# Taking the moments of two of four norms, a product and four casts off VectorE in a kernel with attention, a state-space block and a mixture of experts

## The chip, the cores and the metric

One core of one Trainium2 chip. The metric is the device time of one execution in microseconds (us). VectorE is called DVE here, ScalarE ACT, GpSimd POOL, TensorE PE and SyncE SP, as in the profile.

## The reference

For B = 8 batches of T = 512 rows with D = 256 numbers, and a context of G = 1024 rows with 192 numbers:

```
x  = x + tanh(g_xattn) * block1(layernorm(x), context)
x  = x + tanh(g_ffn)   * block2(layernorm(x))
block1: scores = (t Wq)(c Wk)^T / sqrt(32), 4 heads; the 32 largest of each row's 1024 are kept,
        softmax over them, mean over the heads, times c Wv -> c_t
        y = layernorm(t) * (1 + gate*scale_in(c_t)) + gate*shift_in(c_t)
        y = s4d(y), a long convolution, done with a DFT; then scale_out, shift_out; xt = t + y
        xt = xt + gelu(layernorm(xt) W1 + b1) W2 + b2;  block1 = layernorm(xt)
block2: logits = h Wg; the best of 8 experts and its sigmoid score
        routed = silu(h*score G_e) * (h*score U_e) D_e ;  shared = silu(h G) * (h U) D ; sum of both
```

## The kernel before, in words

A batch is four groups of 128 rows with four heads each, so attention has 128 steps of a group and a head ("attention step" n, 16 a batch). One attention step is, on PE, two score matmuls into two PSUM banks (L1606, L1607); on DVE, four times MAX8 (the eight largest of 1024) and MATCH_REPLACE8 (strike them out), L1301 to L1312; on ACT, small operations, then two exponentials of 128x1024, of all scores and of what is left after the striking; on POOL, the difference of the two and its sum over the heads (L669, L671, L673).

The rest of a batch is "post": FILM_IN (film from c_t), FOLD and DFT, the spectrum's product on DVE (L1443 to L1446) and POOL, INV, FILM_OUT, norm, UP, gelu, DOWN, norm, residual, norm, GATE (the router's logits), RANK (each row's place in its expert's list), the scatter of the rows to xs_d, and SHARED with SH_DOWN (the shared expert), whose result POOL adds to the output by a DMA with accumulation (L835). Post of batch b runs under the attention of batch b + 1. After batches 2 to 6 POOL computes a table of full tiles of routed rows (`tables`, some 35 small operations, L841 to L865), and 21 such tiles run under the attention that follows and under the last post (`tiles`); the 18 that are left run at the end (`routed`), out of expert weights that by then lie in SBUF. `prep` normalizes the next batch's rows and makes queries and keys.

There are four norms a batch: one in `prep`, three in `post`. DVE takes mean and variance (`moments`: four L1275, four L1278), ACT and POOL make the root with a Newton step, ACT applies it.

Each engine runs its instructions in order. That order is written out by hand: every part is a generator that yields the slot, a number, of its next piece, and `weave` merges the parts of one engine by slot. One batch is 128 slots, an attention step 8 slots, one of DVE's eight operations one slot. `post_at(b)` is 128(b+1); the tables ahead of the kernel (DVE_SPECTRUM, POOL_SH, ACT_SILU, POST_AT and others) hold the slots within a batch. A slot is an order only: what holds an instruction is its semaphores. Pieces of equal slot run in the order of the parts in `weave`.

PSUM banks 4 to 7 are a ring (RING, sorted by PE's slots) that post, prep, finish and tiles share; banks 0 to 3 hold the scores.

Around the change, in the order of the slots of one batch on each engine:
- DVE: moments of prep at 56, of post at 55.6 (from L1448 on), 98.6 and 110.1; the router's first part at 118 (waits for GATE, L1468, and ends in `v_hot`), the second at 120.2 (waits for RANK, L1478, and ends in `v_pos`; the four casts of row numbers, L1485, lie in it); the shared product `big[k] = big[k] * bank`, four times, at 126.3 to 132.3 (L1500).
- PE: GATE 123.5, the first SHARED 124, RANK 125.1 (L1848 to L1851), SHARED up to 133 (L1870, eight uses of a bank, two matmuls each), SH_DOWN 134.9 to 138.3 (L1879).
- POOL: ROUTE 117.8, 120.5 (four scalings, L821), 121.6 (four scatters, L828); attention's sums of steps 14 and 15 at 123.3 and 124; `tables` at 133; the four L835 at 133.3 to 134.5; the next batch's first difference at 133.8.
- The difference of step n must be done before DVE's first MATCH_REPLACE8 of step n + 2 (`taken`).
- POOL's FOLD waits until the four L835 of the batch before have landed. In the tail POOL also issues eight scatters of zeros (L912), which the routed tiles' loads wait for.

## Time and profile before

| what | before |
|---|---|
| median of 3 runs | 1889.0 us (1885.12 to 1889.39) |
| profiled execution, its own time | 1896.48 us |
| its span | 1894.6 us |
| granted clock of PE, mean | 0.832 of full speed |
| DVE busy | 1568.8 us, 83% |
| PE busy | 1431.8 us, 76% |
| POOL busy | 1188.9 us, 63% |
| ACT busy | 1043.2 us, 55% |

The span divides in three: to 264 us the convolution's kernel is computed beside the first attention steps; to 1613 us attention goes on, one batch about every 189 us; from there to the end there is the tail: the last post to 1780 us, and the 18 last tiles of the routed experts. The views below give busy time by stretch, what each engine waited for, and single instructions in order of time. A number in square brackets at the end of a timeline row is idle time of the engine before the row, with what ended it.

### The profile page before, as it was taken

What the parts mean: (1) busy time and instruction counts of PE and PEld (TensorE: products, weight loads), DVE (VectorE), ACT (ScalarE), POOL (GpSimd) and SP (SyncE); (2) the same over time, 40 slices, a digit from 0 to 9 for tenths busy, and PEclk for the clock granted to TensorE, in tenths of its full rate; (3) what the DMA queues carried; (4) which work ended last, traced back from release to release, by engine and by line L of the source; (5) the groups of instructions that cost most, each with busy time, mean ns of one, the idle gap of its engine ahead of it and who ended that gap; (6) DMA issues with size and microseconds to landing.
All of it is one profiled execution on the core that took longest, in us unless ns stands there. A gap on an engine that the chain in (4) does not pass through costs nothing.

```text
span 1894.6 us, 20729 instructions
## 1 busy us (share of the span) xinstructions
PE 1431.8 (76%) x6301; PEld 1032.0 (54%) x6301; DVE 1568.8 (83%) x2300; ACT 1043.2 (55%) x2108; POOL 1188.9 (63%) x1293
## 2 busy tenths in 40 slices
PE   3532455786878677868988888888888888887997
PEld 1321343555455545545757565656565656656696
DVE  7899999998999899989998999899999999201321
ACT  2656554474647464746576647665766565333342
POOL 1588845655765576558765875687668756733422
PEclk8655666886888588869998998899988897998998
DMA  7200011001100110013223231323132201472322
GB/s 231 66 3 3 20 32 34 23 16 47 39 23 17 45 39 23 17 45 100 73 59 84 76 89 31 85 75 89 31 84 67 70 17 56 111 267 84 78 47 26
DMA packets 99219, 114.77 MB, mean 61 GB/s; under 512 B 18786, under 2 KB 77930, under 8 KB 98964
## 3 DMA queue, kind: packets, MB, share of 16 engines
q1 hardware_dynamic: 86964, 98.87, 17.9%
q0 software_dynamic: 12144, 14.58, 4.7%
q8 instruction: 51, 0.84, 0.2%
q14 instruction: 60, 0.49, 0.1%
HBM read 75.08 MB, written 19.58 MB: 50 GB/s over the span
## 4 chain that ended last, share of the span: by engine, by line
DVE 53%; PE 21%; POOL 10%; issue 9%; ACT 5%; DMA 1%; SPq 0%; ACTq 0%; DVEq 0%; POOLq 0%
DVE R L1309 17%; DVE ZB L1312 14%; DVE ZB L1305 6%; DVE R L1301 6%; PE PS L1925 3%; PE PS L1870 3%; PE PS L1780 2%; PE PS L1823 2%; DVE R L1265 2%; POOL ZB L673 2%; POOL ZB L671 2%; ACT ZB L946 2%; DVE R L1275 2%; PE PS L1935 2%; POOL R L841 1%
## 5 line engine op out<-in xcount | busy, mean ns | idle before, releaser
L1309 DVE MAX8 R<-ZB 128x8 f32<-128x1024 f32 x384 | 471.2, 1227 | 12.0
L1312 DVE MATCH_REPLACE8 ZB<-R,ZB 128x1024 f32<-128x1024 f32 x384 | 464.1, 1209 | 0.0
L671 POOL TENSOR_TENSOR ZB<-ZB 128x1024 f32<-128x1024 f32 x96 | 233.5, 2433 | 167.1 <-ACT ZB L946 154.1
L949 ACT ACTIVATE R<-PS 128x512 f32<-128x512 f32 (+6 forms) x378 | 159.9, 454 | 264.9 <-PE PS L1879 59.7
L673 POOL TENSOR_TENSOR ZB<-ZB 128x1024 f32<-128x1024 f32 x96 | 228.1, 2376 | 7.5
L946 ACT ACTIVATE R<-R 128x32 f32<-128x32 f32 (+2 forms) x352 | 95.1, 272 | 204.5 <-DVE R L1309 141.6
L669 POOL TENSOR_TENSOR ZB<-ZB 128x1024 f32<-128x1024 f32 x32 | 77.2, 2411 | 161.6 <-ACT ZB L946 108.3
L1606 PE MATMUL PS<-ZR 97*128 97x512 f32 x128 | 83.9, 656 | 119.6 <-ACT ZB L946 96.1
L1870 PE MATMUL PS<-R 128*128 128x512 f32 x256 | 151.5, 748 | 8.4 <-DVE R L1500 8.4
L1301 DVE MAX8 R<-PS 128x8 f32<-128x1024 f32 x128 | 156.4, 1222 | 1.0 <-PE PS L1607 1.0
L1305 DVE MATCH_REPLACE8 ZB<-R,PS 128x1024 f32<-128x1024 f32 x128 | 155.4, 1214 | 0.0
L952 ACT ACTIVATE R<-R 128x1 f32<-128x1 f32 (+1 forms) x384 | 140.7, 390 | 26.4 <-POOL R L658 21.6
L946 ACT ACTIVATE ZB<-ZB,R 128x1024 f32<-128x1024 f32 x128 | 146.1, 1141 | 8.7 <-DVE ZB L1312 8.7
L946 ACT ACTIVATE ZB<-PS,R 128x1024 f32<-128x1024 f32 x128 | 142.7, 1114 | 4.2
L1823 PE MATMUL PS<-R 128*128 128x256 f32 x512 | 121.7, 391 | 10.1 <-ACT R L949 9.5
L1814 PE MATMUL PS<-R 128*128 128x512 f32 x256 | 124.5, 633 | 6.3 <-ACT R L949 4.1
L1631 PE MATMUL PS<-ZB 128*128 128x192 f32 x512 | 112.2, 384 | 13.7 <-ACT ZB L949 10.8
L1631 PEld LDWEIGHTS PS<-ZB 128*128 128x128 f32 x512 | 106.1, 232 | 21.2 <-issue 10.8
L1823 PEld LDWEIGHTS PS<-R 128*128 128x128 f32 x512 | 99.5, 196 | 27.4 <-ACT R L949 11.1
L1606 PEld LDWEIGHTS PS<-ZR 97*128 97x128 f32 x128 | 28.0, 219 | 152.3 <-ACT ZB L946 78.3
L1870 PEld LDWEIGHTS PS<-R 128*128 128x128 f32 x256 | 58.6, 238 | 77.3 <-issue 65.0
L1898 PE MATMUL PS<-R,ZB 128*128 128x128 f32 x672 | 87.3, 289 | 14.2 <-ACT R L949 8.9
(242 smaller groups left out, 3173.8 us busy)
## 6 DMA issues: line engine op xcount, KB each, us to landing
ZR<-ZR SPq DMA_DIRECT2D x96, 128.0 KB
ZB<-in_L_ffn_rt_gate SPq DMA_DIRECT2D x21, 512.0 KB, 4.0
ZB<-in_L_ffn_rt_up SPq DMA_DIRECT2D x21, 512.0 KB, 4.9
ZB<-in_L_ffn_rt_down SPq DMA_DIRECT2D x21, 512.0 KB, 4.4
R<-in_x SPq DMA_DIRECT2D x16, 512.0 KB, 3.9
ZB<-in_ctx SPq DMA_DIRECT2D x8, 768.0 KB, 4.9
ZR<-ZR SPq DMA_DIRECT2D x192, 32.0 KB, 1.8
R<-xs_d SPq DMA_DIRECT2D x39, 128.5 KB, 2.1
```

The lines of the kernel that those rows point to most:

```text
L671: pool.tensor_tensor(e, e, w, ALU.subtract).then_inc(s.g_att, 1)
L673: pool.tensor_tensor(acc, acc, e, ALU.add).then_inc(s.g_att, 1)
L946: return act.activation(*x, **k)
L949: return act.activation(o, i, ACT.Copy, **k)
L952: return act.activation(o, i, ACT.Identity, **k)
L1301: vec.max(ml[:, 0:8], sc_bank(n)).then_inc(s.v_tk, 1)
L1305: vec.match_replace(w, ml[:, 0:8], sc_bank(n), NEG).then_inc(s.v_tk, 1)
L1309: vec.max(ml[:, 8 * r:8 * r + 8], w).then_inc(s.v_tk, 1)
L1312: vec.match_replace(w, ml[:, 8 * r:8 * r + 8], w, NEG).then_inc(s.v_tk, 1)
L1631: ins = pe.matmul(q_bank("finish", t, 2)[:, 0:192], att[:, g, :], cb[b % 2][:, g, :], start=g == 0, stop=g == 7)
L1823: pe.matmul(q_bank("post", b, DOWN + i)[:, 0:256], big[:, k, i * 128:(i + 1) * 128], w2[:, k, :], start=k == 0, stop=False)
L1870: ins = pe.matmul(q_bank("post", b, use), wt[:, c, k * 128:(k + 1) * 128], tr_post[:, c, :], start=c == 0, stop=c == 1)
```

## The change

1. The moments of prep (from batch 1 on) and of the second norm of post are taken on ACT: a copy with a sum (`accum_out`), the mean, then a Square with the mean as bias and a sum. In post the copies that empty DOWN's banks give the sum. The first batch's prep and the other two norms stay on DVE.
2. The shared product goes to POOL, and its operands are now both in SBUF: ACT copies each up bank there first (`sh_up`, two buffers in xt); SH_DOWN waits for all four products (`g_sh`).
3. The four casts of row numbers go from DVE to POOL, between the scalings and the scatters.
4. The queries' tile is one of 4x768 in place of three of 4x256; where the two halves of a batch lie side by side they are moved by one DMA of 128 KB in place of two of 64 KB, and one DVE cast in place of three sets the row of ones.
5. All slots are new, and the post steps and the four tiles under the last post have slots of their own for the last batch.

```diff
-    return post_at(b + 1) + table[k if n == 5 else (0, 2, 3, 4)[k]][step]
+    return post_at(b + 1) + table[5 + k if p == 4 else k if n == 5 else (0, 2, 3, 4)[k]][step]
...
-POOL_ROUTE = (117.8, 120.5, 121.6)
-POOL_SH = (133.3, 134, 134.2, 134.5)
-ACT_SILU = (126.8, 134)
-ACT_SH = (137.8, 138.7, 141.3, 145.2)
-DVE_SPECTRUM = (29.3, 30.4, 32.3, 33.5)
-DVE_MOMENTS = (55.6, 98.6, 110.1)
-DVE_ROUTE = (118, 120.2)
-DVE_SH = (126.3, 130.1, 131, 132.3)
+POOL_ROUTE = ((118.4, 118.4, 119.9), (128.6, 130.3, 130.3))
+POOL_SH = ((135, 135.1, 136.8, 136.9), (142.7, 142.7, 143.5, 153.5))
+ACT_SILU = ((125.6, 135.3), (118.4, 128.6))
+ACT_SH = ((142.1, 142.1, 145, 145), (154.8, 155.3, 155.9, 156))
+DVE_SPECTRUM = ((33.8, 34, 36.7, 36.9), (22.1, 41, 44.9, 47))
+DVE_MOMENTS = ((55.8, 111.5), (51.8, 83.6))
+DVE_ROUTE = ((117.3, 118.5), (107, 109.5))
...
-SP_POST = (0.9, 94.2, 98.1, 99, 104.6)
+SP_POST = ((32.2, 97.8, 103.6, 103.6, 107.5), (-12, 101.9, 125.9, 147.1, 166.8))
+ACT_SHUP = ((126, 135.1, 136.2, 138.8), (124, 124.3, 126.9, 146.9))
+POOL_SHUP = ((121, 132.3, 132.3, 132.3), (130.5, 130.5, 137.2, 137.2))
+ACT_MOMENTS = (5.9, 15)
...
-                        for half in range(2):
-                            q, lo = qt[(2 * b + half) % 3], 512 + 256 * half
+                        o = 2 * b % 3 * 256
+                        for lo, n in ((0, 512),) if o < 512 else ((0, 256), (256, 256)):
...
@@ POOL, post
-                    moments(st_post[1], s.g_rn)
+                    moments(st_post[1], True, s.g_rn)
...
+                    for i in range(4):
+                        pool.tensor_copy(tmp[i][:, D:XW].bitcast(U32), C["tok"][:, 4 * b + i:4 * b + i + 1]).then_inc(s.g_tok, 1)
...
+            def shared():
+                for b in range(B):
+                    for k in range(4):
+                        yield post_at(b) + POOL_SHUP[b == B - 1][k]
+                        use = SHARED + 4 * (k // 2) + k % 2
+                        on.wait_ge(*q_done("post", b, use))
+                        on.wait_ge(*q_done("post", b, use + 2))
+                        pool.tensor_tensor(big[:, k, :], big[:, k, :], sh_up[k % 2], ALU.mult).then_inc(s.g_sh, 1)
...
@@ ACT
+            def mean_of(q):
+                t, m, v = by_scalar(q)
+                on.wait_ge(own.sem, own.n)
+                own.then_inc(copy(m, t, scale=-1.0 / 4096))
+
+            def spread_of(o, i, q, k, sem):
+                t, m, v = by_scalar(q)
+                on.wait_ge(own.sem, own.n)
+                act.activation(o, i, ACT.Square, scale=1.0 / 16, bias=m[:, k:k + 1], accum_out=v[:, k:k + 1]).then_inc(sem, 1)
+
+            def sum_of(o, i, q, k):
+                return copy(o, i, accum_out=by_scalar(q)[0][:, k:k + 1])
...
+                        yield at + ACT_MOMENTS[0]
+                        on.wait_ge(s.x_in, 16 * b + 16)
+                        on.wait_ge(s.g_rin, b)
...
-                        copy(xt[:, i, :], q_bank("post", b, DOWN + i)[:, 0:256]).then_inc(q_sem("post", b, DOWN + i), 1)
+                        sum_of(xt[:, i, :], q_bank("post", b, DOWN + i)[:, 0:256], st_post[1], i).then_inc(q_sem("post", b, DOWN + i), 1)
...
+            def shared():
+                for b in range(B):
+                    for k in range(4):
+                        yield post_at(b) + ACT_SHUP[b == B - 1][k]
+                        use = SHARED + 4 * (k // 2) + k % 2 + 2
+                        on.wait_ge(*q_run("post", b, use))
+                        on.wait_ge(s.g_sh, 4 * b + k - 1)
+                        on.wait_ge(s.a_ln, 12 * b + 8)
+                        copy(sh_up[k % 2], q_bank("post", b, use)).then_inc(q_sem("post", b, use), 1)
...
@@ DVE
-                for q in qt:
-                    vec.tensor_copy(q[96:97, :, :], ones[96:97, 0:1].unsqueeze(2).broadcast_to([1, H, 256])).then_inc(s.v_ones, 1)
+                vec.tensor_copy(qt[96:97, :, :], ones[96:97, 0:1].unsqueeze(2).broadcast_to([1, H, 768])).then_inc(s.v_ones, 1)
...
-                for b in range(B):
-                    yield prep_at(b)
-                    on.wait_ge(s.x_in, 16 * b + 16)
-                    on.wait_ge(s.g_rin, b)
-                    moments(st_prep, xln[b % 2], s.v_mvx)
+                yield prep_at(0)
+                on.wait_ge(s.x_in, 16)
+                moments(st_prep, xln[0], s.v_mvx)
...
-                    for i in range(4):
-                        own.then_inc(vec.tensor_copy(tmp[i][:, D:XW].bitcast(U32), C["tok"][:, n + i:n + i + 1]))
...
-                            TT(big[:, k, :], big[:, k, :], q_bank("post", b, use + 2), ALU.mult).then_inc(q_sem("post", b, use + 2), 1)
...
@@ PE, shared
-                        for use in (2, 3, 6, 7):
-                            on.wait_ge(*q_done("post", b, SHARED + use))
+                        on.wait_ge(s.g_sh, 4 * b + 4)
```

PE's new slots in batches 0 to 6 are GATE 117.2, RANK 117.8, COUNT 118.1, SHARED 117.8 to 130.2, SH_DOWN 137.7 to 139.9, DFT 40 to 40.4 (before 29.3 to 32.4); step 15's scores lie between GATE and RANK. POOL's new slots for FOLD are 17.9 (before 10.7), for the sums of steps 14 and 15 of a batch 127 and 129.6, for the next batch's first difference 133.1; `tables` stays at 133. In the last batch PE has TURN2 at 109.3 and 116.4, RANK at 119.6, all SHARED at 132.4, SH_DOWN at 138.3 to 142.7; POOL's eight scatters of zeros stay at 133.

## Rows read from the trace of the kernel before

**Rows 1.** The page of the kernel before: part 1 and part 4

```profile
PE 1431.8 (76%) x6301; PEld 1032.0 (54%) x6301; DVE 1568.8 (83%) x2300; ACT 1043.2 (55%) x2108; POOL 1188.9 (63%) x1293
...
DVE 53%; PE 21%; POOL 10%; issue 9%; ACT 5%; DMA 1%; SPq 0%; ACTq 0%; DVEq 0%; POOLq 0%
```

**Rows 2.** Windows of one batch and the tail: us, busy (count) per engine, PEclk, DMA share, GB/s

```profile
1000.90:1190.90 190.00, 162.09 (x683) 116.07 (x682) 177.66 (x259) 120.79 (x255) 135.37 (x164) 0.89 0.26 70
...
1620.90:1781.00 160.10, 134.34 (x555) 94.97 (x555) 26.75 (x93) 46.16 (x86) 73.70 (x130) 0.90 0.48 151
```

**Rows 3.** Waits of DVE inside the batch 1000 to 1190: us, times, longest

```profile
DVE R L1478 <- PE PS L1851: 5.5, 1, 5.5
DVE R L1443 <- PE PS L1780: 1.3, 1, 1.3
...
DVE R L1468 <- PE PS L1833: 0.4, 1, 0.4
```

**Rows 4.** Timeline of DVE in that batch: start, us, engine, line, operation, tiles

```profile
999.75 1.23 DVE L1309 MAX8 R<-ZB 128x8 f32<-128x1024 f32 x1
...
1002.62 0.06 DVE L1312 MATCH_VALUE_LOAD ZB<-R,ZB 128x8 f32 x1
...
1003.91 1.23 DVE L1309 MAX8 R<-ZB 128x8 f32<-128x1024 f32 x1
1005.17 0.09 DVE L1312 MATCH_VALUE_LOAD ZB<-R,ZB 128x8 f32 x1
...
1041.06 0.19 DVE L1478 TENSOR_TENSOR R<-PS,R 128x32 f32<-128x32 f32 x1 [5.51 <-PE PS L1851]
...
1041.57 0.31 DVE L1485 CAST R<-R 128x1 uint32<-128x1 f32 x4
...
1049.11 1.23 DVE L1309 MAX8 R<-ZB 128x8 f32<-128x1024 f32 x1
1050.25 0.67 DVE L1500 TENSOR_TENSOR R<-R,PS 128x512 f32<-128x512 f32 x1
1050.84 0.08 DVE L1312 MATCH_VALUE_LOAD ZB<-R,ZB 128x8 f32 x1
...
1075.67 0.09 DVE L1305 MATCH_VALUE_LOAD ZB<-R,PS 128x8 f32 x1
```

**Rows 5.** Timeline of POOL in that batch, after the ranks

```profile
1041.76 3.65 POOL L821 TENSOR_SCALAR R<-R 128x256 f32<-128x256 f32 x4 [5.76 <-DVE R L1483]
...
1062.23 0.19 POOL L864 COPY R<-R 128x1 f32<-128x1 f32 x1
...
1070.85 0.99 POOL L835 DMA_DIRECT2D out<-R  x1 [0.29 <-ACT R L949]
1071.56 2.68 POOL L669 TENSOR_TENSOR ZB<-ZB 128x1024 f32<-128x1024 f32 x1
```

**Rows 6.** Timeline of POOL in the tail, 1640 to 1800

```profile
1642.17 1.27 POOL L764 TENSOR_TENSOR R<-R 128x512 f32<-128x512 f32 x1
...
1770.97 0.97 POOL L912 DMA_INDIRECT xs_d<-R  x1 [0.30 <-issue]
```

**Rows 7.** Timeline of PE in that batch, gate to ranks

```profile
1031.49 3.76 PE L1870 MATMUL PS<-R 128*128 128x512 f32 x4
...
1040.45 0.57 PE L1851 MATMUL PS<-R 128*128 128x8 f32 x2
```

**Rows 8.** Groups of ACT in that batch, by form: busy us, mean ns | idle before

```profile
L949 ACT ACTIVATE R<-PS 128x512 f32<-128x512 f32 x17 | 9.8, 596 | 12.4 <-PE PS L1651 6.0 <-PE PS L1803 3.1 <-PE PS L1790 2.5
...
L949 ACT ACTIVATE R<-PS 128x256 f32<-128x256 f32 x20 | 7.4, 382 | 12.7 <-PE PS L1879 6.5 <-PE PS L1825 4.0 <-PE PS L1906 2.2
...
L946 ACT ACTIVATION_READ_ACCUMULATOR R<-R 128x1 f32 x16 | 3.0, 186 | 0.0
```

**Rows 9.** Chain of waits from 1600 to 1800: start, us, what

```profile
1632.86 7.93 DMA out<-R
...
1772.11 5.45 PE PS L1879 x24
```

More of the change, by code:

```diff
@@ L347, in flamingo_kernel @@
         qs = [big[:, k, :] for k in range(4, 8)]
+        sh_up = [xt[:, 2 * k:2 * k + 2, :].rearrange("p a b -> p (a b)") for k in range(2)]
         end1 = alloc.top
@@ L406, in q_sem, with queried @@
             return s_q[Q[key][1]]
+        def queried(b):
+            return 192 * sum(2 if 2 * k % 3 == 2 else 1 for k in range(b + 1))
         def taken(n):
@@ L928, in routed @@
                 pool.drain()
-            weave(attention(), kernel_rows(), prep(), keys(), weights(), post(), tables(), tiles(), routed())
+            weave(attention(), kernel_rows(), prep(), keys(), weights(), post(), shared(), tables(), tiles(), routed())
         @block.scalar
@@ L1254, in routed @@
                     act.activation(acts[j % 3], PS[:, 1, :], ACT.Silu).then_inc(s.a_silu, 1)
-            weave(attention(), finish(), prep(), keys(), weights(), kernel_rows(), post(), tiles(), routed())
+            weave(attention(), finish(), prep(), keys(), weights(), kernel_rows(), post(), shared(), tiles(), routed())
         @block.vector
@@ L1581, in routed @@
                         vec.tensor_copy(yts[j % 3], PS[:, 3, 0:256]).then_inc(s.v_yt, 1)
-            weave(setup(), attention(), prep(), weights(), kernel_rows(), post(), shared(), tiles(), routed())
+            weave(setup(), attention(), prep(), weights(), kernel_rows(), post(), tiles(), routed())
         @block.tensor
```

323 lines of the change are left out of this document (171 added, 152 removed), and 5 rows, old and new, of the table POST_AT.

## The prediction

> **What bounds the kernel now.** I began with the page: DVE is busy for 1568.8 us, more than any other engine, and the chain that ended last lies on DVE for 53% [rows 1]. An average hides stages, so next I cut the span at one repeating DVE instruction. A middle batch lasts 190.0 us and DVE is busy in 177.7 of them; PE has 162.1, POOL 135.4, ACT 120.8. In the tail DVE has 26.8 of 160.1 us [rows 2]. So until the last attention step (1613 us) work taken off DVE counts, and after it, it doesn't. The waits of DVE in that batch say what stands beside it: 5.5 us for the ranks (L1478), 1.3 for the DFT, 0.4 for the gate [rows 3]; the other idle time is gaps between single instructions. DVE is the bound, with PE's router answer as its one real stall.
>
> **What leaves DVE.** What an instruction costs is read from start to start, with it and without it in between. A MAX8 and the load behind it lie 1003.91 to 1005.17 apart, 1.26 us. With a norm's eight instructions in between it is 999.75 to 1002.62, 2.87 us: a norm costs 1.61. With a product in between it is 1049.11 to 1050.84, 1.73 us: a product costs 0.47, though its row says 0.67 busy. The four casts are one row of 0.31 us [rows 4]. Until the end of attention this makes: prep of batches 1 to 7, 7 x 1.61 = 11.3; post's second norm of batches 0 to 6, 11.3; products of batches 0 to 5 (those of batch 6 fall behind the last attention step), 24 x 0.47 = 11.3; casts 7 x 0.31 = 2.2. Sum 36 us, or 5.5 in a whole batch. The casts of the queries' ones move as many numbers as before: nothing.
>
> The Trainium skill, "VectorE: DVE Perf Modes", section "The DRAIN you can't avoid", says that the next operation doesn't start before the pipe has emptied behind the last. By that a product would cost at least its 0.67 us, 24 x 0.2 = 5 us more gain in all. The rows show less, since the product's start overlaps the MAX8 ahead of it [rows 4]; they decide, and the sum has 0.47.
>
> **What POOL gets, and when.** POOL is idle for 55 us of a batch [rows 2], but not where the products land. Call R the start of L1478, 1041.06. From 1041.76 POOL works nearly without a pause: scalings, scatters, the sums of steps 14 and 15, the table; one DMA of L835 at 1070.85; at 1071.56 the next batch's first difference, to 1074.24, R + 33.2 [rows 5]. DVE needs that difference for the MATCH_REPLACE8 at 1075.67, R + 34.6 [rows 4]. The slack is 1.4 us. Now all four products (121, 132.3) and the casts come ahead of that difference, and the DMA (135) goes behind it. A product is 128x512 on POOL, 1.27 us by L764 [rows 6]; a cast 0.19 by the copy of one column; the DMA gives 0.7 back [rows 5]. 4 x 1.27 + 4 x 0.19 - 0.7 = 5.1, so the difference ends at R + 38.3. DVE in its turn comes 1.9 us of products and 0.3 of casts sooner, but R has moved from slot 120.2 to 118.5, two operations earlier, which lie behind R now: 2.5. It arrives at R + 34.9. **DVE then waits 3.4 us**, in each batch with a table and attention after it: batches 2 to 5, 4 x 3.4 = 14 us. Batches 0 and 1 have no table and so room. The bounds are 0, if POOL gets to its sums sooner than I count, and twice as much, 27 us, if the products wait for ACT, whose slots for the up copies are 135.1 to 138.8.
>
> **The router's answer.** PE now does RANK right behind GATE and one score pair, no longer behind a SHARED, which took 3.76 us (L1870 at 1031.49) while the hot-row chain ran on DVE; the ranks ended at 1041.0 [rows 7]. They start up to 1.9 us sooner. But DVE has one operation (1.26) in place of two to do meanwhile, and there are 5.8 slots between its norm and GATE in place of 7.9, so the wait for GATE (0.4) should grow by 1 to 2 us. Together I take 0, between -2 and +2 a batch. The DFT has its DVE steps 4 slots later than before: of that wait's 1.3 us [rows 3] all or nothing may go. Taken at 0 as well, since POOL's FOLD moves back by the same 5 us; the end for the range is -9 us over seven batches.
>
> **What ACT gets.** Four up copies at 0.6; eight passes of 128x256 for prep and four for post at 0.38, each with a read of the sum at 0.19, and four such reads more in DOWN's copies [rows 8]: 2.4 + 6.8 + 0.8, with the small means some 10.5 us of a batch. ACT goes from 121 to 131 of some 187. An attention step's exponentials have about nine DVE operations of room before PE needs the bank, 11 us, and a group of four passes holds ACT for 2.3. I cost it at nothing; without the cover it would be up to 2 us for each of three groups a batch. The prep moments wait on ACT for the load of x, queued on SP behind FILM_OUT, slot 55; ACT asks at 61.9.
>
> The queries' moves are fewer and larger; PE needs them a batch later. Nothing.
>
> **The tail.** It has three places. First, batch 6's products stand ahead of its table and so of the four L835 and of FOLD: +5.1. Against it, SP's load of u for the last batch has slot -12 and waits there for FOLD, so 9 MB of expert weights queue behind it in place of in front. They were in flight while the last L835 took 7.93 us to land [rows 9]; without them it may be half: -4. Second, the last products: two of four stand behind the eight zero scatters, the last of which starts at 1770.97 [rows 6], and SH_DOWN, which began at 1772.11 [rows 9], now waits for them: 2 x 1.27 behind 1771.9 and 0.8 of casts, +3.4. RANK without a SHARED ahead gives 1.4 back, and expert picks ahead of ACT's last copies 1.9. Third, the second norm's moments on ACT cost about what they cost on DVE, and of PE's idle time before the last tile's DOWN a little goes: -3. Sum near 0, +1 taken, between -9 and +12; PE is busy for 134 of the tail's 160 us to 1781 [rows 2], so more than that isn't to be had.
>
> **Sum.** 1896.5 (the profiled execution) - 36 + 14 + 1 = 1875.5. The median of the runs lies 7.5 lower: **1868 us**.
>
> **Rivals.**
> Full gain: POOL keeps up, and the stall doesn't come. For it: I count POOL without the few idle us that it has in that stretch, and DVE's products no longer hold PE's banks. Against it: the slack of 1.4 us is a row, and 5.1 us are put in front. 1889 - 36 - 9 (the DFT's wait) and 0 to -9 of the tail: 1835 to 1853, middle 1845. Chance 0.30.
> Forecast, POOL's stretch gives back a third: own range 1855 to 1882, chance 0.45.
> No change: the stall is twice as long and the tail loses: 1889 - 36 + 27 + 9 = 1889. Chance 0.10.
> Slower: the products wait for ACT. The third up copy has slot 136.2 and the fourth 138.8, behind ACT's first step of attention step 16 and beside table loads, while POOL, in order, holds the table, the next difference and the L835 behind product 132.3. The gain of 36 us is gone when each of the four batches stalls for 9 us, 5.6 more than I count; at 13 us, with +10 in the tail, it is 1889 - 36 + 52 + 10 = 1915. For it: three engines take turns with two buffers. Against it: PE ends its SHARED about 20 us behind R, and POOL reaches the products at R + 21 anyway. Chance 0.12.
> That it doesn't do what it says: the square's pass could cost ACT a table load and more per norm; then ACT becomes the late one, the same sign as the last. Chance 0.03, 1900.
>
> **Numbers.** 1868 is the likeliest case. The range takes in the full gain down to 1838 and reaches up to 1893, short of the slow cases: outside are some 0.15 above and 0.05 below. A measurement of this kernel tells apart about 0.3%, 5.7 us. Faster: 0.45 + 0.30 + a part of the middle case, 0.77; same 0.09; slower 0.14.
>
> **What would show it.** In the windows of a middle batch: DVE busy near 172 us, POOL near 141, ACT near 131, a length of 187 with a table and 184 without. In DVE's waits: a new one, L1305 on POOL, of 3 us, once in each of batches 2 to 5; L1478 between 3 and 6. In POOL's timeline: three products of 1.3 right ahead of the table. In the tail: the landing of L835 near 4 us, SH_DOWN behind the last two products. I am wrong about the give-back if L1305 shows no wait, wrong about DVE as the bound if busy falls by 5 us and the batch doesn't, and wrong about ACT if PE's scores wait for its exponentials where DVE waits for the scores.

## The result and the profile after

The changed kernel takes 1902.5 us (median of 10 runs, 1899.5 to 1904.8), the kernel before 1893.1 us in the same runs (10, 1885.1 to 1901.9). The ratio is 1.0049, with a 95% interval of 1.0029 to 1.0070: slower by 9 us. The prediction was 1868, between 1838 and 1893, so it is wrong in sign, and the result lies above its range. Runs of the kernel before fall in two groups, near 1885 and near 1897, and the trace shown of it is one of the upper group; so times are compared by the ratio to the runs of before made beside them, and a difference of two traces against it understates a loss, and overstates a gain, by up to some 10 us.

The page of the changed kernel, parts 1 and 4, to be read against [rows 1]:

```profile
PE 1423.8 (75%) x6301; PEld 1031.4 (54%) x6301; DVE 1523.8 (80%) x2114; ACT 1098.6 (58%) x2359; POOL 1230.1 (65%) x1357
...
DVE 41%; PE 23%; POOL 13%; ACT 11%; issue 9%; DMA 2%; SPq 0%; POOLq 0%; ACTq 0%; DVEq 0%
```

DVE lost 45 us of busy time, ACT and POOL gained 55 and 41, as the offload says. But the share of the last chain that lies on DVE fell from 53% to 41%, and what left it went to PE, POOL and ACT. Windows of the changed kernel, one batch and the tail, columns as in [rows 2]:

```profile
1025.06:1215.51 190.45, 159.83 (x675) 116.50 (x676) 172.20 (x234) 128.65 (x288) 140.26 (x171) 0.89 0.26 70
1620.90:1781.00 160.10, 128.25 (x520) 92.30 (x519) 21.50 (x74) 49.01 (x97) 76.84 (x130) 0.88 0.46 146
```

DVE is busy for 172.2 us (172 forecast), POOL 140.3 (141), ACT 128.7 (131): the loads came out as forecast. The batch didn't: 190.5 us, not 187. DVE's waits in it, from 1016 to 1215 (the gate's line has two waits there, one of each batch), answer to [rows 3]:

```profile
DVE R L1544 <- PE PS L1896: 7.9, 2, 4.0
DVE R L1554 <- PE PS L1914: 5.1, 1, 5.1
DVE ZB L1387 <- POOL ZB L694: 3.3, 3, 1.7
DVE R L1383 <- PE PS L1670: 1.2, 1, 1.2
```

The gate (L1544) costs 4.0 us where it cost 0.4, the ranks (L1554) 5.1 for 5.5, and the DFT's wait is gone. POOL's differences (L1387) cost 3.3 in three waits; the one that was forecast, at the next batch's first difference, is the longest of them, 1.7 us and not 3.4.

To place the loss I cut both kernels' traces at R, DVE's read of the ranks (L1478 before, L1554 after), which comes once a batch. R(0) is batch 0's. Under R(0) to R(2) there are no tiles, under R(2) to R(6) there are, and R(6) to R(7) is the last post:

| us | to R(0) | to R(2) | to R(6) | to R(7) | to the end |
|---|---|---|---|---|---|
| before | 475.3 | 375.7 | 750.0 | 149.3 | 144.3 |
| after | 466.5 | 367.5 | 760.4 | 157.4 | 148.9 |
| difference | -8.8 | -8.2 | +10.4 | +8.1 | +4.6 |

By these traces the change gains 4.1 us a batch where there are no tiles, loses 2.6 where there are, and loses 12.7 behind R(6).

### The profile page after: what moved, and what is told of

It is laid out like the page before. It is cut to its first block, busy times and chain, and to the rows that moved or that the text cites. A ratio compares the mean times of both kernels' runs of the same rounds, so it can differ in the third digit from the quotient of the medians.

```text
span 1900.7 us, 20831 instructions
## 1 busy us (share of the span) xinstructions
PE 1423.8 (75%) x6301; PEld 1031.4 (54%) x6301; DVE 1523.8 (80%) x2114; ACT 1098.6 (58%) x2359; POOL 1230.1 (65%) x1357
## 4 chain that ended last, share of the span: by engine, by line
DVE 41%; PE 23%; POOL 13%; ACT 11%; issue 9%; DMA 2%; SPq 0%; POOLq 0%; ACTq 0%; DVEq 0%
DVE R L1391 14%; DVE ZB L1394 11%; DVE ZB L1387 5%; DVE R L1383 4%; ACT ZB L983 3%; PE PS L1989 3%; ACT R L989 2%; POOL ZB L696 2%; PE PS L1962 2%; POOL ZB L698 2%; PE PS L1877 2%; PE PS L1886 1%; PE PS L1896 1%; ACT R L986 1%; PE PS L1970 1%
## 5 line engine op out<-in xcount | busy, mean ns | idle before, releaser
L696 POOL TENSOR_TENSOR ZB<-ZB 128x1024 f32<-128x1024 f32 x96 | 231.6, 2413 | 107.2 <-ACT ZB L983 107.0
L986 ACT ACTIVATE R<-PS 128x256 f32<-128x256 f32 (+5 forms) x410 | 176.4, 466 | 183.2 <-PE PS L1853 38.8
L989 ACT ACTIVATE R<-R 128x1 f32<-128x1 f32 (+1 forms) x384 | 141.3, 390 | 30.8 <-POOL R L683 26.2
L1387 DVE MATCH_REPLACE8 ZB<-R,PS 128x1024 f32<-128x1024 f32 x128 | 155.5, 1215 | 0.0
L1935 PE MATMUL PS<-R 128*128 128x512 f32 x256 | 134.4, 675 | 1.5 <-ACT R L986 1.5
L1877 PE MATMUL PS<-R 128*128 128x512 f32 x256 | 126.6, 640 | 9.9 <-ACT ZB L986 4.7
L1962 PE MATMUL PS<-R,ZB 128*128 128x128 f32 x672 | 98.1, 312 | 32.3 <-issue 14.5
L1694 PE MATMUL PS<-ZB 128*128 128x192 f32 x512 | 106.3, 369 | 20.7 <-ACT ZB L986 12.5
L986 ACT ACTIVATE ZB<-PS 128x512 f32<-128x512 f32 (+2 forms) x97 | 47.4, 500 | 121.6 <-PE PS L1687 70.0
L1694 PEld LDWEIGHTS PS<-ZB 128*128 128x128 f32 x512 | 99.3, 221 | 33.4 <-issue 19.3
L1962 PEld LDWEIGHTS PS<-R,ZB 128*128 128x128 f32 x672 | 95.9, 227 | 39.7 <-issue 31.2
L1886 PE MATMUL PS<-R 128*128 128x256 f32 x512 | 116.5, 379 | 0.9 <-ACT R L1242 0.9
```

The lines of the kernel that those rows point to most:

```text
L696: pool.tensor_tensor(e, e, w, ALU.subtract).then_inc(s.g_att, 1)
L986: return act.activation(o, i, ACT.Copy, **k)
L989: return act.activation(o, i, ACT.Identity, **k)
L1387: vec.match_replace(w, ml[:, 0:8], sc_bank(n), NEG).then_inc(s.v_tk, 1)
L1694: ins = pe.matmul(q_bank("finish", t, 2)[:, 0:192], att[:, g, :], cb[b % 2][:, g, :], start=g == 0, stop=g == 7)
L1877: ins = pe.matmul(q_bank("post", b, UP + k), w1[:, c, k * 128:(k + 1) * 128], tr_post[:, c, :], start=c == 0, stop=c == 1)
```

## The experiments

Slots named are those of batches 0 to 6 unless a text says otherwise.

### New code in the old order, old code in the new order

```diff
@@ the changed kernel
-POST_AT = ((15.3, ...
+POST_AT = (13.8, 21.3, ...          and so every table of slots, for all batches
+ACT_SHUP = (127.2, 127.5, 134.2, 134.5)
+POOL_SHUP = (126.3, 130.1, 131, 132.3)
+ACT_MOMENTS = (5.9, 6.2)
```

> The changed kernel's operations in the order of the kernel before: every slot table as it was, the last batch without slots of its own, the new pieces put where DVE's product lay (product on POOL at 126.3 to 132.3, up copies on ACT behind the silus they follow, moments of prep right ahead of their root). Theory S (the offload gains, the new order gives it back): DVE busy some 45 us less than in the kernel before, attention ends at least 20 us sooner, and the time is near 1870, 1.0 to 1.5% below the kernel before. Theory O (the work put on POOL and ACT costs what DVE gains, in any order): 1890 or more, with DVE's waits on POOL and on PE's scores grown by 4 us or more a batch.

Ratio 1.0441 (1.0409 to 1.0473), 1973 us. Theory O's "1890 or more" covers that in the letter, but neither theory expected a loss of 84. R(2) to R(6) is 797 us, with DVE waiting 58 us for scores in all. These slots for the new pieces were mine, so the run shows only that the new pieces don't fit the old order as it stands.

```diff
@@ the kernel before
-POST_AT = (13.8, 21.3, ...
+POST_AT = ((15.3, ...               and so every table, with the last batch's own slots
+DVE_MOMENTS = ((55.8, 101.9, 111.5), (51.8, 66, 83.6))
```

> The other half: the kernel before, its operations unchanged, in the new order, the last batch's own slots among it (DVE's middle moments at 101.9 and its products at 126.3 to 132.3). Theory S: the new order alone makes the kernel before slower by 20 us or more, 1913 and up, with DVE's waits for the gate near 3.5 us and for the ranks near 5 in every batch, and the tail some 6 us longer. Theory O: the order is neutral or better, 1880 to 1895. If both this and the new code in the old order are faster than the kernel before, neither alone is at fault and it is how they meet on POOL.

Ratio 1.0184 (1.0154 to 1.0215): the new order alone costs the old code 35 us. The offload then brings 1.0184 down to 1.0049, 26 us. So both halves are now measured along this path: the order loses 35 us, and the offload gains 26 in it (21 by the medians, 1923.8 and 1902.5). Along the other path, with the new pieces' slots placed by hand, they don't add. The traces, which have +26 and -20 for the two steps, divide them so, in us:

| | to R(0) | to R(2) | to R(6) | to R(7) | to the end |
|---|---|---|---|---|---|
| the order, old code | -6.5 | -0.2 | +21.8 | +3.3 | +7.4 |
| the offload, new order | -2.3 | -8.0 | -11.4 | +4.9 | -2.8 |

The order costs nothing where there are no tiles, and 5.4 us in each batch that has them. DVE is busy for 709 us between R(2) and R(6) in both kernels, so what grew is idle time. Its waits there, the kernel before first (851.5 to 1601.5 us), then this run (845 to 1617):

```profile
DVE R L1478 <- PE PS L1851: 13.5, 4, 5.5
DVE R L1468 <- PE PS L1833: 3.0, 3, 2.0
```

```profile
DVE R L1472 <- PE PS L1845: 20.4, 4, 5.1
DVE R L1462 <- PE PS L1827: 14.5, 4, 3.9
```

The ranks (first lines) and the gate (second lines) cost 18.4 us more over four batches. POOL's differences add 5.1 and the scores 3.4, and the DFT's waits, 6.0 us before, are gone. In the two batches without tiles, gate and ranks together cost 3.0 us more and the DFT 3.8 less. The 5.5 us that I had read for the ranks in the middle batch was no constant either: in the three batches after it the kernel before waits 4.4, 2.3 and 1.3 us. The new order waits 5.1 in each.

### The suspected stall of POOL

```diff
-                    yield post_at(b) + 133
+                    yield post_at(b) + 133.15     # POOL, tables()
```

> The changed kernel with POOL's table of full tiles moved from slot 133 to 133.15, just behind the next batch's first difference (133.1). If POOL's stretch ahead of that difference is what gives the gain back, DVE's wait for POOL at its first MATCH_REPLACE8 (10.7 us over the run) goes, attention ends 10 us sooner and the time falls by 8 to 11 us, to about 1893. The rival: that wait is only the last of a set that end close together (scores, ranks), so 3 us or less of it comes back and the time stays within 1899 to 1903.

1.0153 (1.0122 to 1.0183), slower than the changed kernel by 1%. The 10.7 us of the expectation were ten waits for first differences of a group of rows; the four at the next batch's first difference, some 37 us behind R, are 2.3, 1.7, 1.1 and 1.0. These four did go. But DVE's waits for the other differences (L696) grew from 0.9 to 15.2, R to POOL's FOLD from 51.3 to 55.6 us in the batches with a table, and R(2) to R(6) from 760 to 776. The stall I had found is real and small, and it isn't what a batch is made of.

```diff
-                        pool.tensor_tensor(big[:, k, :], big[:, k, :], sh_up[k % 2], ALU.mult).then_inc(s.g_sh, 1)
+                            TT(big[:, k, :], big[:, k, :], q_bank("post", b, use + 2), ALU.mult)   # DVE again, 126.3 to 132.3
```

> The changed kernel with the shared product back on DVE, out of PSUM, at the slots it had there (126.3 to 132.3; in the last batch at 129); ACT's up copies and POOL's products are gone; the moments and the casts stay where the change put them, and all other slots are the new ones. If POOL's stretch is the give-back, POOL's table and difference come 3.8 us sooner, DVE's wait at its first MATCH_REPLACE8 (10.7 us over the run) falls to 2 or less, DVE takes 11 us of products back, and the two about cancel in attention; the tail gains 5 us since nothing waits behind the zero scatters: 1895 to 1900. If the product on POOL is a plain gain, this run is slower than the changed kernel by 8 us or more, 1910.

1.0023 (1.0000 to 1.0047). R(2) to R(6) is 760.1 (760.4): four products a batch on DVE or on POOL, it makes no difference there. The product's price was right: the MAX8 ahead of it starts at 1034.81 and the load behind it at 1036.55, 1.74 us, a product 0.48 above the pair without one, as in [rows 4]; the Trainium skill, "VectorE: DVE Perf Modes", section "The DRAIN you can't avoid", would by its first statement have at least the 0.67 of its row, and the trace again shows less; the section adds that an operation that isn't held starts earlier, with which the overlap agrees. Where the gain went stands in POOL's timeline of this run:

```profile
1254.53 2.35 POOL L685 TENSOR_TENSOR ZB<-ZB 128x1024 f32<-128x1024 f32 x1 [4.50 <-ACT ZB L963]
```

POOL, 3.8 us lighter, now waits 4.5 us for an exponential, which in its turn comes behind DVE's MAX8s. R to FOLD is 49.8 us in the first batch with a table (51.9) and 51.2 to 51.5 in the others (51.3 to 51.5). With a table, POOL's stretch and DVE's own end together, and moving the product is worth nothing. Without one POOL has room, and there the product off DVE gains 0.2 to 0.9 us a batch and not 1.9; what takes the rest is open.

### Filling the waits

```diff
-DVE_ROUTE = ((117.3, 118.5), ...
+DVE_ROUTE = ((119.3, 122.5), ...
```

> The changed kernel with the two parts of DVE's router two and four operations later (slots 119.3 and 122.5 in place of 117.3 and 118.5) in batches 0 to 6. If the waits are idle time that other attention steps can fill, the wait for the gate falls from 3.7 to about 1.2 us and that for the ranks from 5.1 to about 2.6, 5 us a batch in seven batches: attention ends about 30 us sooner and the time is 1870 to 1880. The rival: the waits are PE's own pace (165 of 190 us busy), so they come back elsewhere in the same batch as waits for scores or for POOL, and the time stays at 1900.

1.0063 (1.0038 to 1.0088), as the changed kernel. DVE's timeline of this run:

```profile
1017.33 0.19 DVE L1532 COPY R<-PS 128x32 f32<-128x32 f32 x1 [1.53 <-PE PS L1884]
...
1024.88 0.19 DVE L1542 TENSOR_TENSOR R<-PS,R 128x32 f32<-128x32 f32 x1 [2.51 <-PE PS L1902]
...
1038.49 1.23 DVE L1371 MAX8 R<-PS 128x8 f32<-128x1024 f32 x1 [6.08 <-PE PS L1658]
```

Both waits shrank exactly as meant, 2.5 us each, and came back as 6.1 us for scores that PE issues behind SHARED.

```diff
+PE_SCORES = (-9.8, ...             # and the router as above
```

> The run before this one (route later) with one thing more: PE's scores of the next batch's first step are issued at slot 118.2, right behind RANK, instead of at 127.8, behind four uses of SHARED. In the route-later run DVE waited 6.1 us for these scores, which PE did at 1037.4, though their bank was free at 1021.6. If PE's order is what holds the waits in place, 6 us a batch come free, DVE's wait for scores falls back to 1 us and the time goes below 1880. If POOL's stretch (products, table, difference) is what ends last behind it, the wait moves a third time, to DVE's first MATCH_REPLACE8 behind that difference: 3 to 6 us more there in each batch with a table, and the time is 1890 to 1902.

1.0038 (1.0017 to 1.0059). The scores' wait is gone (1.8 us left in all), and DVE waits for POOL's sum of step 14, which stands behind the scatters, as the rival said. The view is DVE's waits from 300 to 1600 us:

```profile
DVE ZB L1375 <- POOL ZB L684: 34.0, 6, 6.1
DVE R L1542 <- PE PS L1902: 17.5, 7, 2.5
```

### Undoing the moments

```diff
+                for b in range(B):                 # DVE, prep(): at prep_at(b), slot 56
+                    moments(st_prep, xln[b % 2], s.v_mvx)
+                    moments(st_post[1], xt, s.v_mv)   # DVE, post(): at 101.9
```

> The changed kernel with the moments of prep and of post's second norm back on DVE (prep at slot 56, post at 101.9; in the last batch at 66), ACT's sums gone; product and casts stay on POOL, all other slots are the new ones. DVE gets 22.6 us of work back by attention's end, 3.2 us a batch. Theory D (DVE's load sets the batch, as forecast): the time grows by 15 to 22 us, to 1918 to 1925. Theory L (the ring over POOL and PE sets it, and DVE only waits for the gate and the ranks): DVE's wait for the gate shrinks by as much, R to R stays within 1 us of the changed kernel's 183.8 and 191, and the time is within 5 us of 1902.

1.0136 (1.0109 to 1.0163) against 1.0049: 16 us for 22.6 us of work, near theory D. R to R grew from 183.7 and 183.9 to 186.9 and 186.3, by 2.8 of 3.2 us, and with tiles from 190.1 to 192.8 in the mean. DVE's work does count, though DVE waits 9 us in each batch. Theory L is wrong as stated, and so is what it expected of the next run.

```diff
-POOL_TILE = ((37,), ... (161.6,), ...
+POOL_TILE = ((30.2,), ... (146.1,), ...
```

> Theory L: a batch is as long as the ring R to R (R is DVE's read of the ranks), which runs over POOL and PE, not over DVE's load: R to FOLD, then FOLD to R. In the changed kernel FOLD to R is 134.2 us in batches without tiles and 139.3 with them (before the change 142.2 in both), because two scatters of tile rows (POOL slots 161.6, which is 33.6 of the next batch, and 37) stand between INV and FILM_OUT, the second waiting 1.1 us for the first to land. This run moves them to 146.1 (right behind FOLD) and 30.2, nothing else. L expects FOLD to R to fall by 2.5 to 4 us in each of batches 4, 5 and 6, and the time by 6 to 12 us, to 1891 to 1897. The rival (DVE's queue of work and waits sets the batch) expects no change beyond 2 us, since DVE does the same.

1.0059 (1.0036 to 1.0082): nothing, as the rival said. FOLD to R, 138.9 and 139.7 us in batches 4 and 5 of the changed kernel, is 139.7 and 139.8.

```diff
@@ both edits: the product on DVE, POOL_TILE as above
```

> Two edits together: the product back on DVE (alone it gave 1896.9 in its run, 5 us of it in the tail) and the two scatters of tile rows at 146.1 and 30.2. If the two gains lie in different places (tail, FOLD to R), they add: 1896.9 less 6 to 12 us, 1885 to 1891, below the kernel before. If they overlap, 1893 to 1897.

1.0053 (1.0031 to 1.0075); no gain to add.

### The tail

```diff
-POST_AT = (..., (13.4, 14.3, ...       every table's entry for the last batch
+POST_AT = (..., (15.3, 15.3, ...       as for the other batches
```

> The changed kernel with the last batch and its four tiles on the slots of the other batches (only the last tile's scatter on POOL is at 139.7, as before the change). Attention up to step 124 should be as in the changed kernel. If the last batch's own slots lose the tail (theory: the load of u at -12, the two last products behind the zero scatters, RANK at half clock), the time falls by 5 to 10 us, to 1893 to 1898. If they are worth something, as their place in the order of weights and tiles says, the tail gets longer, by 5 us or more: 1908 and up, and then the tail's loss is in the offloaded work itself.

1.0238 (1.0206 to 1.0270). R(6) to FOLD is 76.8 us for 44.8: next to the new order the last batch needs slots of its own.

```diff
-ACT_SHUP = (..., (124, 124.3, 126.9, 146.9))
-POOL_SHUP = (..., (130.5, 130.5, 137.2, 137.2))
+ACT_SHUP = (..., (124, 124.3, 126.9, 141.9))
+POOL_SHUP = (..., (130.5, 130.5, 132.9, 132.9))
```

> The changed kernel with the last batch's two last products at slot 132.9 on POOL, in front of the eight scatters of zeros (133), and the fourth up copy at 141.9 on ACT, in front of the first expert pick. If SH_DOWN's wait of 8.4 us is due to the products standing behind the zero scatters, SH_DOWN starts 5 to 8 us sooner, the first routed gate comes 3 to 5 us sooner and the time falls by as much, to 1898. If the routed part waits for the scatters or the picks anyway (they now come 2.5 us later), nothing is gained: 1901 to 1905.

1.0055 (1.0037 to 1.0072). SH_DOWN starts 7.3 us sooner, and the first routed gate at 1789.5, not 1786.5. PE's timeline of the changed kernel, and then of this run:

```profile
1777.42 7.07 PE L1943 MATMUL PS<-R 128*128 128x256 f32 x24 [8.40 <-POOL R L872]
...
1786.49 3.74 PE L1989 MATMUL PS<-R 128*128 128x128 f32 x32
```

```profile
1770.13 5.47 PE L1931 MATMUL PS<-R 128*128 128x256 f32 x24 [2.10 <-POOL R L860]
...
1785.19 0.47 PE L1966 MATMUL PS<-R 128*128 128x128 f32 x1 [9.60 <-DMA R<-xs_d]
```

The products, and 3.6 us that POOL waits for the last up copy ahead of them, pushed the zero scatters back by 5.2 us, and the rows for the first tile load behind these. PE waits 9.6 us for the rows, and then it needs 4.3 us at a granted clock of 0.50 for the transposes and the last SH_DOWN ahead of the gate, which took 2.2 at 1.00 in the changed kernel. So most of the 3.0 us is the clock. Either order on POOL delays one of the two.

```diff
+            def shared():                     # DVE, b = B - 1 only, at 129
+                    TT(big[:, k, :], big[:, k, :], q_bank("post", b, use + 2), ALU.mult)
```

> The changed kernel with the product of the last batch alone on DVE, which is idle there (slot 129), batches 0 to 6 as changed. In the changed kernel's tail SH_DOWN waits 8.4 us for the last two products, which POOL does behind the eight scatters of zeros. With all products off POOL the zero scatters start at the landing of the row scatters and SH_DOWN is done before the first rows land. Theory: the tail after the ranks shortens by 2 to 3 us, and the time is 1898 to 1901. If the product on DVE run owed its 5 us to the batches before instead, nothing is gained: 1902.

1.0014 (1.0001 to 1.0028), below the changed kernel's 1.0049. R(7) to the end is 145.2 us for 148.9: 3.7 of the 4.6 us lost there are the last products on POOL (2.2 by the run with all products on DVE, 146.7).

### The chain ahead of the ranks

What holds DVE at the gate is a chain of single latencies. DVE's moments of the third norm end (M), then come ACT's root, POOL's Newton step, ACT's norm, PE's turn, ACT's copies, PE's GATE, the gate's read on DVE, PE's RANK, and R. The changed kernel on DVE, and then on PE:

```profile
1017.52 0.19 DVE L1544 COPY R<-PS 128x32 f32<-128x32 f32 x1 [3.98 <-PE PS L1896]
...
1018.63 0.19 DVE L1352 TENSOR_TENSOR R<-R 128x32 f32<-128x32 f32 x1
1018.74 1.22 DVE L1391 MAX8 R<-ZB 128x8 f32<-128x1024 f32 x1
1025.06 0.19 DVE L1554 TENSOR_TENSOR R<-PS,R 128x32 f32<-128x32 f32 x1 [5.10 <-PE PS L1914]
```

```profile
1011.93 1.26 PE L1866 MATMUL PS<-R 128*128 128x128 f32 x8 [3.22 <-ACT R L989]
1013.93 3.55 PE L1896 MATMUL PS<-R 128*128 128x8 f32 x16 [0.73 <-ACT R L986]
...
1018.88 0.60 PE L1911 MATMUL PS<-R 128*128 128x8 f32 x2 [0.35 <-DVE R L1352]
```

Between the gate's answer and the ranks DVE has one operation to do, a MAX8; before the change it had two, and between moments and gate it had 7.9 slots for 5.8.

```diff
-ACT_ROOT = ((61.5, 101.9, 115.4), ...
-ACT_REST[12] = 16.4
+ACT_ROOT = ((61.5, 101.9, 112.3), ...
+ACT_REST[12] = 16.2
```

> The changed kernel with ACT's root of the third norm at slot 112.3 in place of 115.4 in batches 0 to 6, ahead of the two exponentials of the next attention step (the second exponential of the step before goes to 112.2, to stay ahead of it). In the changed kernel DVE's moments end at 1004.89, ACT takes the root at 1007.26, behind those exponentials, and DVE reads the gate at 1017.52, having waited 4.0 us. Theory W (the stretch from the moments to the ranks is a chain of latencies, in which DVE has only seven operations to do, so every us of it is a us of the batch): the gate and the ranks come 2 us sooner, DVE's wait for the gate falls from 3.7 to 1.7, R to R falls by 2 us and the time by 10 to 14, to 1888 to 1892. Theory Q (some queue behind R sets the batch, as when the router was moved): the wait moves on, R to R is unchanged and the time within 3 us of the changed kernel's.

1.0125 (1.0092 to 1.0158): slower, since the edit did the opposite of what I meant. ACT's timeline of this run:

```profile
817.67 0.54 ACT L971 ACTIVATE R<-R 128x4 f32<-128x4 f32 x2 [6.45 <-DVE R L1349]
...
819.40 1.11 ACT L971 ACTIVATE ZB<-PS,R 128x1024 f32<-128x1024 f32 x1
820.41 1.14 ACT L971 ACTIVATE ZB<-ZB,R 128x1024 f32<-128x1024 f32 x1
821.45 2.07 ACT L977 ACTIVATE R<-R 128x256 f32<-128x256 f32 x4
```

The two exponentials got in between root and norm. M to the gate's read went from 11.0 to 12.2 us, and R to R from 183.8 to 184.8. Runs whose code is the same up to R(2) have 183.1 to 183.8 us there, so a difference of 0.5 us is at the edge of what one trace tells.

```diff
+DVE_MOMENTS = ((55.8, 110.5), ...    # 111.5 before; root as above, the last product on DVE
```

> The run before with two edits more: DVE's moments of the third norm one operation earlier (110.5; their input is ready 2.8 us before they start), and the last batch's product on DVE (worth 3.5 us alone). Under W each is a gain of its own: another 1.2 us in each of seven batches and 3 us in the tail, 11 us below the run before, 1877 to 1881, and below the kernel before the change by some 0.7 to 1%. Under Q only the tail's 3 us are gained.

1.0058 (1.0037 to 1.0080); R to R 183.5 and 183.0.

```diff
+ACT_NORM = ((62.7, 112.35), ...      # 117.4 before; the rest as in the run before
```

> The run with the last batch's product on DVE (1899.0), with the third norm done first: DVE's moments one operation earlier (110.5), and on ACT both its root (112.3) and its norm (112.35) ahead of the two exponentials of the next attention step, which in the root-earlier run had slipped in between root and norm and made the latency from moments to gate 1.2 us longer, and R to R 1.2 us longer with it (183.7 to 184.9). Theory W: in batches without tiles the latency is 11.0 us again and R to R falls by the one operation, to 182.5; in batches with tiles the latency falls from 13 to 11, and R to R from 191 to 188. Together 12 to 17 us: 1883 to 1888, a ratio near 0.993. If in the batches with tiles POOL's stretch from R to FOLD, which has no idle time, takes what is won, R to R stays at 190.5 there and only 5 us are gained: 1894.

1.0133 (1.0102 to 1.0164). The exponentials now hold up the copies: M to gate is 12.9 us without tiles and 17.5 to 18.2 with them, R to R 184.3 and 194.2.

```diff
+DVE_ROUTE = ((119.3, 122.5), ...
+PE_SCORES[0] = -9.8
+ACT_MAX[14], ACT_EXP[14], ACT_REST[14] = 11.6, 11.65, 11.65
+ACT_ROUTE = ((123.8, 126.8), ...
+POOL_SUM[14] = 6
```

> The run before, with the router later on DVE (119.3 and 122.5) and this time all four queues moved with it: PE's scores of the next batch's first step at 118.2, ACT's exponentials of step 14 at 123.65, ahead of the router's, POOL's sum of step 14 at 118, ahead of the scalings. Moving the router alone sent the wait to PE's scores (6.1 us), moving the scores too sent it to POOL's sum of step 14 (6.1 us). If nothing else stands in the way, DVE does four operations more inside the chain of latencies: its waits for gate and ranks fall by 5 us a batch and stay gone, POOL's stretch from R to FOLD is 4.7 us shorter, R to R falls by 3 to 5 us and the time to 1860 to 1870. If a fifth queue takes the wait (ACT's table loads and silus behind the ranks, or POOL's first difference), R to R falls by less than 1 us and the time stays at that of the run before.

1.0122 (1.0090 to 1.0153), no better than the run before. Without tiles R to FOLD did fall by 4.5 us (49.4 to 44.9), and FOLD to R grew by 4.0 (134.8 to 138.8); DVE waited for scores again, 20.8 us in all.

```diff
+ACT_ROOT = ((61.5, 101.9, 112.3), ...
+ACT_REST[13] = 13.5                  # its second exponential behind the norm, which is at 117.4 again
+DVE_MOMENTS = ((55.8, 110.5), ...    # ACT_REST[12] = 16.2 and the last product on DVE as before
```

> The run with the last batch's product on DVE (1899.0), the third norm's moments one operation earlier (110.5) and its root at 112.3, as in the two runs before; new is where ACT's work of the attention step goes: the first exponential between root and norm, while POOL does the Newton step (2 us), the second behind the norm (117.5), while PE turns. Rule so far, from two runs: R to R changes by the change of the latency from moments to gate less 1.25 us for the operation that moved behind the moments. Here the latency should be 11.0 in batches without tiles (R to R 182.5, from 183.8) and 11.7 in those with tiles, where POOL's difference of step 12 ends 2.6 us behind the moments (R to R 189 to 190, from 191). The time by that is 8 to 12 us below the last-product run, 1888 to 1891, a ratio of 0.996 to 0.998. If the latency is 12 or more again, R to R is 184 and 191 and nothing is gained.

1.0054 (1.0030 to 1.0077). Without tiles the chain is 11.2 us and R to R 182.5 and 181.8, as the rule says. With tiles it is 14.2, and R to R 191.1. The four runs against the rule, without tiles, per batch; it was drawn from the first ones, and only the last was forecast by it:

| run | change of M to gate | operation moved | rule | R to R measured, from 183.8 |
|---|---|---|---|---|
| root earlier | +1.2 | no | +1.2 | +1.0 |
| and moments earlier | +1.2 | yes, -1.25 | 0 | -0.5 |
| and norm earlier | +1.9 | yes | +0.6 | +0.5 |
| exponentials in the gaps | +0.2 | yes | -1.1 | -1.7 |

The rule holds within 0.6 us. So a batch without tiles fits the chain together with DVE's work outside it. With tiles the rule fails for a shorter chain, and the traces say where a longer one starts. The changed kernel, first DVE and PE, then ACT and POOL:

```profile
1184.78 0.74 DVE L1609 SCALAR_TENSOR_TENSOR R<-PS,R 128x512 f32<-128x512 f32 x1
...
1185.63 3.75 PE L1970 MATMUL PS<-ZB,R 128*128 128x256 f32 x8 [4.48 <-issue]
...
1193.42 1.15 ACT L983 ACTIVATE ZB<-ZB,R 128x1024 f32<-128x1024 f32 x1
...
1194.65 2.36 POOL L694 TENSOR_TENSOR ZB<-ZB 128x1024 f32<-128x1024 f32 x1 [4.41 <-ACT ZB L983]
...
1198.50 0.23 POOL L679 TENSOR_SCALAR R<-R 128x4 f32<-128x4 f32 x1 [1.49 <-ACT R L983]
```

PE stands for 4.5 us in front of a tile's last product, until DVE has done the tile's own multiplication (slot 105.9, L1609). Behind it come, in order, PE's transposes, ACT's copies of them, the exponential, POOL's difference, and only then POOL's Newton step. In batches 4 and 5, from that multiplication to R it is 30.7 and 30.9 us in the changed kernel, 31.0 twice with the root earlier, 30.7 and 30.8 with the moments earlier, 30.5 twice with the exponentials in the gaps, though M moved by 1.3 us among them. Before the change it was 32.3 and 30.2, with 17.4 slots of attention in it (102.8 to 120.2) against 12.6 now (105.9 to 118.5). At 1.26 us a slot that leaves 10.4 and 8.3 us uncovered before, and 14.8 and 15.0 now: 4 to 7 us more. The old code in the new order agrees: 30.9 and 31.3 us, so 15.0 and 15.4 uncovered, and batches of 193.0 us for 187.5. In batch 6 the four runs differ (28.3 to 31.8). That the tile's multiplication starts the chain is read from traces that agree; no run moved it alone.

### One part alone

```diff
@@ the kernel before, ACT and POOL
-                        copy(xt[:, i, :], q_bank("post", b, DOWN + i)[:, 0:256])
+                        copy(xt[:, i, :], q_bank("post", b, DOWN + i)[:, 0:256], accum_out=...)
+                        spread_of(tmp[i][:, 0:D], xt[:, i, :], st_post[1], i, s.a_sum)
-                    moments(st_post[1], xt, s.v_mv)          # DVE
```

> The kernel before with one part of the change alone: the moments of post's second norm on ACT (sums out of DOWN's copies, then mean and four squares ahead of the root at 103.1), every slot as before, all else as before. DVE loses 1.61 us a batch until attention's end, 11.3 us. If work off DVE counts in any order, as the moments' undo says (20 of 22.6 us in the new order), R to R falls by 1.3 to 1.6 us from 187.9 and 189 and the time by 8 to 11 us, a ratio of 0.994 to 0.996 to the kernel before: that would be faster than both kernels. If ACT's squares (2.3 us at once) delay an exponential that DVE or PE waits for, R to R is unchanged and the ratio 1.000 or above.

1884.9 us, ratio 0.9990 (0.9965 to 1.0016). Its trace is shorter than that of before by 14 us, but the runs of this kernel spread from 1878 to 1896 us, and the trace is of a run at 1882.5. By the ratio it isn't told apart from no change, and the 8 to 11 us that I expected lie outside the interval, which ends at a gain of 7. No version that I ran is shown to be faster than the kernel before; the last product on DVE (1.0014) is the best of the new order.

## Why the prediction was wrong

**DVE as the bound, and the terms of its work.** Right in size for the norms: 1.61 us each, 22.6 in all, and the undo gives 16 by ratio and 2.8 of 3.2 us a batch by R. The product's 0.47 us was right as a price. I took it off DVE as 11.3 us and charged 14 for the stall that it brings, so my sum had it at a small loss up to the end of attention; the runs put the two together at zero (1128.1 us from R(0) to R(6) with it on DVE, 1127.9 on POOL). This term didn't fail.

**POOL's stall.** It came where I put it and at under half its size: 2.3, 1.7, 1.1 and 1.0 us in the four batches with a table and attention behind, 6 us for my 14. The difference ends at R + 37.5 to 36.9, where I had 38.3, and DVE arrives at R + 35.3 to 35.9, where I had 34.9.

**"Together I take 0": the router's answer.** This is the step that failed. Up to R(6) the traces have the offload at -21.7 us in the new order, and I had -36 + 14 = -22: the moved work came out as forecast. What the sum lacked is the new order itself, +35 us for the old code by ratio, of which I had costed only the router and the DFT, at 0, and some pieces of the tail. In the batches with tiles DVE's waits for gate and ranks grew together by 4.6 us a batch, where I had 0, between -2 and +2.

I had both parts, the ranks 1.9 us sooner and the gate's wait 1 to 2 us longer, and let them cancel. They aren't of one kind. Without tiles, the ranks' earlier start shortens the chain from M to R from 20.7 us to 18.6. The slots taken out of it, 10.1 before and 7.0 after, are 3.9 us of DVE's work moved to where the chain doesn't cover it. That is 1.8 us lost, and the DFT's wait of 1.9, now gone, hides it: the order alone leaves these batches at 187.8 us. With tiles the chain starts earlier, 12.6 slots ahead of R, and there it loses 4 to 7 us a batch. Nor are the ranks sooner there: from M to R it is 20.9, 19.8, 17.6 and 17.5 us before, and 20.2, 20.6, 20.8 and 18.2 after, where PE does the gate, and in the last two also the ranks, at half the clock in the new order (last section). The whole new order is shown to cost 35 us, and these waits are where it shows; how much of it is the moved slots and how much the clock, no run isolates.

**The DFT's wait.** It went but for 1.8 us once, and was 1.9 us a batch without tiles and 1.5 with them, the good end of my range; I had taken 0.

**ACT at nothing.** In the changed kernel DVE's waits that name ACT are 0.8 us in all from 300 to 1600 us, so that holds as it stands. But the cover is thin: exponentials that got into the chain made it 1.2 to 1.9 us longer without tiles, up to 5 with them, and the batch with it.

**The tail.** I took +1 and it is +12.7 from R(6) on. Batch 6's products cost 3.4 us (R(6) to FOLD is 39.9 before, 44.8 after, 41.4 with the product on DVE), and the 4 us that I gave back for L835's landing didn't come. The last products behind the zero scatters cost 3.7, forecast 3.4. FOLD to R(7) grew by 3.3, against the 3 us of gain that I had there; the old code in the new order has 1.9 of it. By the two halves the order costs 10.7 us from R(6) on and the offload 2.1.

**The rivals.** "No change" came nearest, and for other reasons: twice the stall wasn't needed. The slower rival, products waiting for ACT, is not what happened: POOL waits 0.4 us for an up copy in the middle batch, 0.9 in an early one. It waited 3.6 us for one only where the last products were moved forward.

## What to carry to other kernels

An engine that is busy for over 90% of a stage and still waits may be bound by a chain of latencies through it: cost a move by where it lies against that chain, since work taken out of the chain's shadow gains nothing and work moved out of it costs its full length. Where an order is written by hand, cost the new order as a change of its own, by counting how many operations each waiting stretch holds before and after. Read such a wait in more than one batch: the ranks cost 5.5 us in the one that I read and 1.3 in another. And where two engines' stretches end together, a unit of work moved from one to the other gains nothing, however exactly its price is known.

## What the runs showed of the chip

PE's clock in the chain. Windows over the changed kernel's GATE and its RANK, then over GATE before the change (us, busy and count of PE, PEld, DVE, ACT, POOL, then granted clock, DMA share, GB/s):

```profile
1013.93:1017.30 3.37, 3.37 (x16) 3.37 (x17) 0.00 (x0) 0.00 (x0) 3.29 (x2) 0.50 0.71 157
1018.88:1024.80 5.92, 5.92 (x28) 5.92 (x28) 1.08 (x1) 4.15 (x10) 0.23 (x1) 0.50 0.61 136
```

```profile
1029.32:1031.49 2.17, 2.17 (x16) 2.17 (x17) 1.88 (x2) 0.13 (x1) 2.09 (x2) 0.82 0.56 125
```

The same 16 matmuls take 3.4 us at a granted clock of 0.50, the 1.2 GHz level, and 2.2 us at 0.82. Ahead of the slow one PE had stood idle for 3.2 us before its turn (1011.93, above); before the change it had stood for 1.0 us at most there. RANK does the same in the last two batches with tiles. Its windows in batch 5, before the change and after:

```profile
1412.89:1416.13 3.24, 3.24 (x29) 3.14 (x27) 1.00 (x1) 0.60 (x1) 1.44 (x1) 0.99 0.37 40
```

```profile
1400.29:1406.25 5.96, 5.96 (x28) 5.96 (x29) 1.08 (x1) 4.14 (x10) 0.22 (x1) 0.50 0.61 135
```

It is the order that does this, and not the offload. GATE's row in batches 3 to 6 is 2.3, 1.9, 1.9 and 1.9 us in the kernel before, and 1.9 in each with the new code in the old order. It is 3.6 in all four in the changed kernel, and 3.4 to 3.6 with the old code in the new order. In the three batches ahead of these it is 3.6 in all four kernels. For the four batches with tiles that makes 6 us in GATE and, in two of them, 5 in RANK: by its size half of the 21.8 us that the order costs there, an estimate from these rows, since no run changed the clock alone. I hadn't counted that an order which leaves PE idle ahead of the gate makes the gate itself slower.

And Square with a sum took no table load of its own: the loads are 117 in the changed kernel and 121 before, and a square of 128x256 is a row of 0.50 us with a read of 0.19 behind it.
